# Edge keys as DRAM rows instead of PE transposes, in a two-layer graph kernel on one core

## The chip, the cores and the metric

The program runs on one core of a Trainium2 chip, as one launch. The metric is the time of that launch in device microseconds (us). The time of the kernel before is the median of three runs, 2639.05 us (2638.74 to 2639.62).

## The reference, cut to what matters

Two blocks follow each other on `x` (1250 nodes, 768 features). Each adds to `x` the output of a two-layer graph attention network (GAT) and of a token mixer, both fed by a layer norm of `x`, and then the output of a feed-forward part with chosen experts.

```python
xn = _layernorm(x)
x = x + gnn0(xn, edge_index, ...) + mix0(xn, ...)     # gnn0: 2 GAT layers, 4 heads
x = x + ffn0(_layernorm(x), ...)                      # 2 experts out of 4 for all nodes
xn = _layernorm(x)
x = x + gnn1(xn, edge_index, ...) + mix1(xn, ...)     # gnn1: 2 GAT layers, 1 head
x = x + ffn1(_layernorm(x), ...)
```

A GAT layer does `e = leaky_relu(a_src[src] + a_dst[dst])`, a softmax of `e` over the edges that share a `dst`, and a weighted sum of `h[src]`. There are 21250 edges, `src` and `dst` being int32 arrays of that length, drawn at random, with repeats. The kernel turns the edge list once into a dense matrix of counts (how often an edge occurs), and does every softmax and sum with that matrix.

## The kernel before, in words

Nodes are cut into NT = 10 tiles of T = 125. All five engines run programs of their own, written out in order, and wait for each other on semaphores. PSUM has two rings of banks: five that VectorE (DVE) drains (list `V`) and three that ScalarE (ACT) drains (list `A`); `plan()` writes both lists, and PE and the draining engine walk them in the same order. A bank is filled again only when its entry five (or three) places earlier has been drained.

The start. SP (SyncE's queue) loads `x` in five pieces of two tiles (L2336 to L2341), the value weights W in two halves, the edges as two tiles of 125 partitions by 170 integers, and stores zeros from SBUF over the two count matrices in DRAM (L2346 to L2348). DVE takes the norm's statistics of each piece and normalises it (L1419 to L1432; piece 2 is normalised only after the statistics of piece 3, piece 3 after those of piece 4). PE turns each pair of tiles (L573) and multiplies it with the first half of W (products `("v", t, 0)`), then all tiles with the second half (`("v", t, 1)`). DVE drains the first two products only after piece 4 (L1428 to L1431).

The edge list. An edge's key is `src * 1250 + dst`. The 21250 keys form 170 columns of 125. DVE makes the keys (L1437 to L1440). A scatter with repeated indices would lose additions, so each column is first searched for repeats. For that every partition needs the whole column as a row: PE turns the column, broadcast over 125 columns, into PSUM (`key_rows`, L560 to L568; four columns fill a bank, so there are 43 groups). DVE then compares the row with its own key, once for each column (L1456), which gives how often the key occurs and whether it is the first. Every five groups (20 columns) DVE makes indices and counts (L1469 to L1475) and signals `index_made`. GpSimd (POOL) then adds each column into one of the two count matrices with an indirect DMA, in order, with at most two in flight (L2287 to L2294). It starts only when the zeros are written (L2285).

The 43 groups stand between other PE work: 5 beside the first half of the products v, 12 beside the second (KEYS_BESIDE), 6 in the first block of q and k (KEYS_BESIDE_QK), and 4 after each of heads 0 to 4 (KEYS_AFTER_HEAD).

Then come the eight mixer heads (pk, pq, kv, in some of them a further block of q and k, then num), while POOL scatters. After the heads PE turns the result and makes the first half of GAT layer 0's product (`("h", 0, t, 0)`, L657). For the next stage SP waits until all scatters have landed (L2440), loads the counts (L2443 to L2451), DVE sums them (`count_sum`, L1597 and L1599), and PE turns them into the mask (`mask(j)`, L637) beside the mixer's output product.

The end of GAT layer 1. `gat4` accumulates for each head over ten source tiles j into five banks (L717 to L733). In the last head of layer 1 the last four j are taken bank by bank (L735 to L744, `by_pairs`), so that bank 0 is complete first; in all other heads j is the outer loop. DVE drains a bank, takes statistics, ACT normalises pair by pair (`normalise`, L1041), and PE turns the result for the feed-forward part.

Of the kernel before, what the change touches and what calls it, by code (L numbers as in the profile page):

```python
# [20 lines left out]
F32 = mybir.dt.float32  # L21
# [34 lines left out]
KEYS_BESIDE = [0] * 6 + [2, 3] + [1] * 12  # L56
KEYS_BESIDE_QK = [1] * 6
KEYS_AFTER_HEAD = [4] * 5 + [0] * 3
# [34 lines left out]
def plan():  # L93
# [29 lines left out]

    turned("ln0", range(5))
    keys = [("key", i) for i in range(NKEY)]

    def some_keys(n):
        for _ in range(n):
            V.append(keys.pop(0))

    for half in range(2):
        for t in range(NT):
            V.append(("v", t, half))
            some_keys(KEYS_BESIDE[half * NT + t])

    def qk(b):
        for i, x in enumerate("kq"):
            for c in range(3):
                V.append((x, b, c))
                if b == 0:  # L140
                    some_keys(KEYS_BESIDE_QK[3 * i + c])

    qk(0)
    for h in range(MH):
# [6 lines left out]
        some_keys(KEYS_AFTER_HEAD[h])  # L151
    assert not keys
# [57 lines left out]
def gps_kernel(nc, w, out):  # L210
# [8 lines left out]
    neg_dram = nc.dram_tensor("neg_saved", [T, NT * N], BF16).ap()  # L219
    prow_dram = [nc.dram_tensor(f"target_rows{i}", [2, (H0 - 1) * NT, T], F32).ap() for i in range(2)]  # L220
# [5 lines left out]
    with ctx:  # L226
# [109 lines left out]
        SRCI, DSTI = in_d(EC).bitcast(I32), in_d(EC).bitcast(I32)  # L336
        SRCF, DSTF, KEY, COUNT, FIRSTF, IDXE = (in_d(EC) for _ in range(6))
# [109 lines left out]
        pair_stats, pair_std, pair_normed = sem("pair_stats_made"), sem("pair_std_made"), sem("pair_normed")  # L447
        keys_made, index_made = sem("keys_made"), sem("index_made")
# [57 lines left out]
        def _(pe):  # L506
# [51 lines left out]
            keys = list(range(NKEY))  # L558

            def key_rows():  # L560
                i = keys.pop(0)
                pe.wait_ge(keys_made, 1)
                b = fill("V", ("key", i))
                for j in range(min(KEYG, EC - i * KEYG)):
                    c = i * KEYG + j
                    last = pe.transpose(b[0:T, j * T:(j + 1) * T], KEY[0:T, c:c + 1].to_broadcast([T, T]),
                                        IDENT[0:T, 0:T])
                last.then_inc(v_filled, 1)  # L568

            for half in range(2):  # L570
                for t in range(NT):
# [5 lines left out]
                    for _ in range(KEYS_BESIDE[half * NT + t]):  # L577
                        key_rows()

            def qk(blk):  # L580
                pe.wait_ge(qkw_loaded[blk % 2], 48 * (blk // 2 + 1))
                for i, x in ((1, "k"), (0, "q")):
                    for c, (n0, n) in enumerate(CH):
# [4 lines left out]
                        if blk == 0:  # L588
                            for _ in range(KEYS_BESIDE_QK[3 * (1 - i) + c]):
# [2044 lines left out]
```

## Time and profile before

| | |
|---|---|
| median of 3 runs | 2639.05 us |
| the profiled execution | 2642.76 us, span 2641.0 us |
| PE busy | 2567.0 us (97%) |
| DVE busy | 1586.7 us (60%) |
| ACT busy | 779.6 us (30%) |
| POOL busy | 347.4 us (13%), nearly all of it the 170 scatters |
| DMA | 155.70 MB, mean 59 GB/s |

The profiled execution took 2642.76 us, of which the profile covers 2641.0 us. Times in the rows are us from the start of the span. The view of groups gives for each the busy time, the mean ns of one instruction, and the idle time of the engine just before them with what ended it.

### The profile page before, as it was taken

What the parts mean: (1) busy time and instruction counts of PE and PEld (TensorE: products, weight loads), DVE (VectorE), ACT (ScalarE), POOL (GpSimd) and SP (SyncE); (2) the same over time, 40 slices, a digit from 0 to 9 for tenths busy, and PEclk for the clock granted to TensorE, in tenths of its full rate; (3) what the DMA queues carried; (4) which work ended last, traced back from release to release, by engine and by line L of the source; (5) the groups of instructions that cost most, each with busy time, mean ns of one, the idle gap of its engine ahead of it and who ended that gap; (6) DMA issues with size and microseconds to landing.
All of it is one profiled execution on the core that took longest, in us unless ns stands there. A gap on an engine that the chain in (4) does not pass through costs nothing.

```text
span 2641.0 us, 26830 instructions
## 1 busy us (share of the span) xinstructions
PE 2567.0 (97%) x10673; PEld 1821.8 (69%) x10673; DVE 1586.7 (60%) x2708; ACT 779.6 (30%) x1314; POOL 347.4 (13%) x197
## 2 busy tenths in 40 slices
PE   7999999999999997999999999999999999999999
PEld 4667667558965987777777775465755786556676
DVE  4456471789948996997788998254432461341322
ACT  1043342016732873222222221430002431342000
POOL 0888888000000000000000000000000000000000
PEclk9999999999999998999999999999999999999999
DMA  9232313543020406000120002200350100213201
GB/s 255 23 46 14 50 2 49 142 124 104 20 60 0 106 11 214 1 0 1 72 100 2 24 24 85 99 1 0 97 182 18 36 0 1 59 35 131 86 24 59
DMA packets 138070, 155.70 MB, mean 59 GB/s; under 512 B 96524, under 2 KB 108390, under 8 KB 136418
## 3 DMA queue, kind: packets, MB, share of 16 engines
q1 hardware_dynamic: 67225, 153.56, 18.8%
q0 software_dynamic: 70720, 0.43, 2.8%
q8 instruction: 84, 1.38, 0.2%
q14 instruction: 41, 0.34, 0.0%
HBM read 117.75 MB, written 35.83 MB: 58 GB/s over the span
## 4 chain that ended last, share of the span: by engine, by line
PE 51%; DVE 7%; ACT 2%; issue 1%; DMA 0%; SPq 0%; DVEq 0%; ACTq 0%
PE psum L523 50%; DVE arena L1878 2%; DVE arena L1880 1%; DVE arena L1879 1%; PE psum L534 0%; DVE arena L1871 0%; ACT arena L1140 0%; ACT arena L1145 0%; ACT arena L1031 0%; DVE arena L1536 0%; DVE arena L1944 0%; DVE arena L1378 0%; DVE arena L1877 0%; DVE arena L1870 0%; DVE arena L1903 0%
## 5 line engine op out<-in xcount | busy, mean ns | idle before, releaser
L523 PE MATMUL psum<-arena 128*125 128x384 f32 (+12 forms) x9762 | 2459.8, 413 | 39.0 <-DMA arena<-in_ffn_w 7.1
L523 PEld LDWEIGHTS psum<-arena 128*125 128x125 f32 (+3 forms) x9762 | 1721.0, 188 | 751.5 <-issue 136.4
L2293 POOL DMA_INDIRECT count_matrix<-arena x170 | 342.8, 2016 | 122.8 <-DVE arena L1475 60.9
L1878 DVE RECIPROCAL arena<-arena 128x500 f32<-128x500 f32 x60 | 196.7, 3278 | 2.1
L1628 DVE CUSTOM_DVE_ANT_0 arena<-arena 125x1250 bf16<-125x1250 bf16 (+1 forms) x100 | 139.2, 1457 | 12.9 <-ACT arena L1173 12.3
L2303 POOL MEMSET arena<- 125x60 f32 x1 | 0.2, 207 | 1047.0 <-PE psum L523 1047.0
L1712 DVE TENSOR_TENSOR arena<-arena 125x1250 f32<-125x1250 f32 x80 | 116.3, 1453 | 18.5 <-ACT arena L1122 18.3
L1119 ACT ACTIVATE arena<-arena 125x1250 f32<-125x1250 f32 x80 | 106.9, 1336 | 54.5 <-PE psum L523 54.2
L1715 DVE SCALAR_TENSOR_TENSOR arena<-arena 125x1250 f32<-125x1250 f32 x80 | 116.9, 1461 | 2.8
L1031 ACT ACTIVATE arena<-psum 128x250 f32<-128x250 f32 (+1 forms) x102 | 40.6, 495 | 231.9 <-PE psum L534 231.5
L1265 ACT ACTIVATE arena<-psum,arena 128x250 f32<-128x250 f32 x120 | 49.3, 465 | 198.3 <-PE psum L523 198.3
L1074 ACT ACTIVATE arena<-arena 32x500 f32<-32x500 f32 (+1 forms) x108 | 59.1, 548 | 164.8 <-DVE arena L1509 163.9
L1122 ACT ACTIVATE arena<-arena 125x1250 f32<-125x1250 f32 x80 | 105.8, 1322 | 0.0
L1164 ACT ACTIVATE arena<-psum 125x384 f32<-125x384 f32 x80 | 38.6, 487 | 139.7 <-PE psum L523 139.7
L1257 ACT ACTIVATE arena<-arena 128x500 f32<-128x500 f32 x60 | 37.2, 621 | 140.1 <-DVE arena L1862 139.9
L534 PE MATMUL psum<-arena 125*128 125x125 f32 x420 | 57.7, 282 | 20.1 <-DVE arena L1397 11.3
L1140 ACT ACTIVATE arena<-arena 125x250 f32<-125x250 f32 x100 | 40.4, 490 | 116.5 <-PE psum L523 116.4
L1734 DVE TENSOR_TENSOR arena<-arena 125x2500 f32<-125x2500 f32 x10 | 27.6, 2764 | 72.8 <-ACT arena L1145 72.8
L534 PEld LDWEIGHTS psum<-arena 125*128 125x128 f32 x420 | 45.5, 143 | 33.5 <-issue 19.4
L1646 DVE TENSOR_SCALAR arena<-arena 125x40 f32<-125x40 f32 (+1 forms) x4 | 0.7, 178 | 106.5 <-ACT arena L1164 78.3
L1507 DVE TENSOR_SCALAR arena<-psum,arena 96x500 f32<-96x500 f32 (+1 forms) x36 | 23.3, 647 | 66.0 <-PE psum L523 65.6
L1862 DVE TENSOR_SCALAR arena<-arena 128x500 f32<-128x500 f32 x60 | 25.0, 420 | 60.5 <-ACT arena L1265 59.1
(223 smaller groups left out, 1463.9 us busy)
## 6 DMA issues: line engine op xcount, KB each, us to landing
arena<-in_ffn_w SPq DMA_DIRECT2D x3, 4608.0 KB, 15.4
residual<-arena SPq DMA_DIRECT2D x30, 336.0 KB
arena<-residual SPq DMA_DIRECT2D x30, 336.0 KB
arena<-target_rows SPq DMA_DIRECT2D x12, 610.4 KB
arena<-in_gat_w SPq DMA_DIRECT2D x3, 2304.0 KB, 9.4
arena<-residual SPq DMA_DIRECT2D x10, 672.0 KB
residual<-arena SPq DMA_DIRECT2D x10, 672.0 KB
count_matrix<-arena SPq DMA_DIRECT2D x2, 3125.0 KB, 27.0
```

The costliest lines, as they stand in the source:

```text
L523: return pe.matmul(o, lhsT, rhs, start=start, stop=stop, skip_group_check=share)
L534: last = pe.transpose(b[:, i * T:(i + 1) * T], source[0:T, t0 + i, k * 128:(k + 1) * 128], IDENT[0:T, 0:T])
L1031: act.activation(o, i, ACT.Copy).then_inc(a_drained, 1)
L1074: act.activation(o[low, cols], t[32 * i:32 * i + 32, cols], ACT.Square)
L1119: act.activation(ET4[n % 4][0:T, :], PROWS[layer][h % 2][0][0:T, :], ACT.Exp, bias=ASC[0:T, h, j:j + 1])
L1122: act.activation(E24[n % 2][0:T, :], PROWS[layer][h % 2][1][0:T, :], ACT.Exp, bias=AS2[0:T, h, j:j + 1]).then_inc(slopes_made, 1)
L1265: last = act.activation(HB[u % 2][:, m, :], b[:, j * 250:(j + 1) * 250], ACT.Identity, bias=B1C[:, e, m:m + 1])
L1628: ins = dve.tensor_tensor_reduce(SUMS[n % 2][0:T] if layer < 2 else E24[n % 2][0:T, :], NEG[0:T, t, :], ASROWS[layer][h % 2][0:T, :], 1.0, ...
L1712: dve.tensor_tensor(et, et, E24[n % 2][0:T], ALU.max).then_inc(larger_made, 1)
L1715: dve.scalar_tensor_tensor(et, et, 1.0, CT[0:T, j, :], ALU.min, ALU.mult).then_inc(et_made, 1)
L1878: now(dve.reciprocal(t_, t_))
L2293: pool.indirect_dma_start(counts[k], bass.IndirectOffsetOnAxis(ap=IDX_I[0:T, c:c + 1].bitcast(U32), axis=0), COUNT_I[0:T, c:c + 1], None, ...
```

## The change

Four things are changed.

1. The keys are made in row form. The edges are loaded first of all, as 170 rows of 125 in two parts (128 and 42 partitions), and DVE makes the keys in this form (KEYT) before it looks at `x`. PE turns KEYT once (two transposes), DVE copies the result to the column form KEY that the compares need.
2. KEYT is stored to DRAM (`key_rows`), and each group of four rows is read back by all 125 partitions with one broadcast DMA of up to 250 KB, into one of two buffers in SBUF. The 170 transposes of `key_rows` on PE go away, and DVE compares with a row in SBUF instead of one in PSUM. A load of group i waits until group i - 2 has been used. These loads stand between SP's other loads.
3. The order of SP's first loads is new: edges, x0, first half of W, x1, bias row, KEYT stores, x2, zeros of matrix 0, key rows of groups 0 and 1, x3, zeros of matrix 1, x4, second half of W. The groups are spread differently over DVE's work (5 in the first half of v as before, but beginning two tiles earlier, 7 in the second half, 6 in the first q and k block, 4 after each of heads 0 to 5, 1 after head 6), and the index batches become 2 groups, then ten times 4, then 1.
4. In the last head of GAT layer 1 the order by pairs is gone; it runs as the other heads do. ACT's wait for the last bank moves from pair 3 to pair 0.

```diff
-KEYS_BESIDE = [0] * 6 + [2, 3] + [1] * 12
+KEYS_BESIDE = [0] * 4 + [1, 1] + [1, 1, 1, 0, 1, 1, 0, 1, 1, 0, 1, 1, 0, 1]
 KEYS_BESIDE_QK = [1] * 6
-KEYS_AFTER_HEAD = [4] * 5 + [0] * 3
+KEYS_AFTER_HEAD = [4] * 6 + [1] + [0]
+KEY_BATCHES = [2] + [4] * 10 + [1]
@@ PE
-            def key_rows():
-                i = keys.pop(0)
-                pe.wait_ge(keys_made, 1)
-                b = fill("V", ("key", i))
-                for j in range(min(KEYG, EC - i * KEYG)):
-                    c = i * KEYG + j
-                    last = pe.transpose(b[0:T, j * T:(j + 1) * T], KEY[0:T, c:c + 1].to_broadcast([T, T]),
-                                        IDENT[0:T, 0:T])
-                last.then_inc(v_filled, 1)
+            pe.wait_ge(keyt_made, 1)
+            b = fill("V", ("keyt",))
+            pe.transpose(b[0:T, 0:128], KEYT[:, 0, :], IDENT)
+            pe.transpose(b[0:T, 128:EC], KEYT[0:EC - 128, 1, :], IDENT[0:EC - 128, 0:EC - 128]).then_inc(v_filled, 1)
...
-                    by_pairs = 4 if (layer, h) == (1, H0 - 1) else 0
-                    for j in range(NT - by_pairs):
+                    for j in range(NT):
@@ ACT
-                if stage == 1 and g == 3:
+                if stage == 1 and g == 0:
                     act.wait_ge(v_filled, V_AT[("acc", 1, H0 - 1, 4)] + 1)
@@ DVE
+            dve.wait_ge(edges_loaded, 64)
+            for i, p in parts:
+                step(dve.tensor_copy(SRCTF[p, i, :], SRCT[p, i, :]))
+                step(dve.tensor_copy(KEYT[p, i, :], DSTT[p, i, :]))
+            after(own[0])
+            step(dve.scalar_tensor_tensor(KEYT[:, 0, :], SRCTF[:, 0, :], float(N), KEYT[:, 0, :], ALU.mult, ALU.add))
...
             def key_group():
                 i = keys.pop(0)
-                dve.wait_ge(v_filled, V_AT[("key", i)] + 1)
-                b = bank(("key", i))
+                dve.wait_ge(rows_loaded[i % 2], 16 * (i // 2 + 1))
...
-                    row = b[0:T, j * T:(j + 1) * T]
+                    row = KEY_ROWS[i % 2][0:T, j * T:(j + 1) * T]
@@ SP
+            x_load(0)
+            load(W[:, :, 0:HALF], w["mix0_wv"][:, :, 0:HALF], wv_loaded[0])
+            x_load(1)
+            row_load(0, "mix0_bv", bv_loaded)
+            sp.wait_ge(keyt_made, 1)
+            load(key_dram[0:128], KEYT[:, 0, :], keyt_saved)
+            load(key_dram[128:EC], KEYT[0:EC - 128, 1, :], keyt_saved)
+            sp.wait_ge(zeros_made, 1)
+            x_load(2)
+            zeros_store(0)
+            sp.wait_ge(keyt_saved, 32)
+            key_rows_load(0, 2)
+            x_load(3)
+            zeros_store(1)
+            x_load(4)
+            load(W[:, :, HALF:], w["mix0_wv"][:, :, HALF:], wv_loaded[1])
...
+            key_rows_load(2, 14)
             vf(("v", NT - 1, 1))
-            pieces_load(WS8[:, :, 2 * H0:], w["gat1_w"], gw_loaded[1])
+            pieces_load(WS8[:, :, 2 * H0:], w["gat1_w"], gw_loaded[1], lambda k: key_rows_load(14 + k, 15 + k))
...
                 block_load(blk)
+                if blk > 2:
+                    key_rows_load(4 * blk + 8, 4 * blk + 12)
+            key_rows_load(28, 32)
...
             block_load(5)
+            key_rows_load(32, NKEY)
```

## Rows read from the trace of the kernel before

**Rows 1.** The page, parts 1 and 4: busy times, and the chain by engine.
```profile
PE 2567.0 (97%) x10673; PEld 1821.8 (69%) x10673; DVE 1586.7 (60%) x2708; ACT 779.6 (30%) x1314; POOL 347.4 (13%) x197
...
PE 51%; DVE 7%; ACT 2%; issue 1%; DMA 0%; SPq 0%; DVEq 0%; ACTq 0%
```
**Rows 2.** Groups by line, the key transposes: busy us, mean ns, idle before them.
```profile
L566 PE MATMUL psum<-arena 125*125 125x125 f32 x170 | 23.4, 274 | 4.0 <-DVE arena L1562 4.0
```
**Rows 3.** Timeline where PE waits for the counts: start us, us, engine, [idle before].
```profile
64.46 2.14 POOL L2293 DMA_INDIRECT count_matrix<-arena  x1 [60.90 <-DVE arena L1475]
...
83.56 1.98 POOL L2293 DMA_INDIRECT count_matrix<-arena  x1 [0.30 <-issue]
...
467.12 1.99 POOL L2293 DMA_INDIRECT count_matrix<-arena  x1 [0.30 <-issue]
...
477.27 0.29 DVE L1599 TENSOR_TENSOR arena<-arena 125x125 f32<-125x125 f32 x1
...
477.82 1.72 PE L642 MATMUL psum<-arena 125*125 125x125 f32 x10 [2.17 <-DVE arena L1599]
```
**Rows 4.** Timeline of DVE in the first 80 us.
```profile
22.23 1.02 DVE L1378 BATCH_NORM_STATS2 arena<-arena 125x6 f32<-125x384 f32 x2 [2.13 <-DMA arena<-in_x]
...
26.12 1.01 DVE L1378 BATCH_NORM_STATS2 arena<-arena 125x6 f32<-125x384 f32 x2
...
30.33 1.01 DVE L1414 TENSOR_TENSOR arena<-psum,arena 125x384 f32<-125x384 f32 x2
...
62.32 0.18 DVE L1469 TENSOR_SCALAR arena<-arena 125x20 f32<-125x20 f32 x1
...
74.52 0.56 DVE L1414 TENSOR_TENSOR arena<-psum,arena 125x384 f32<-125x384 f32 x1 [2.68 <-PE psum L523]
...
76.06 0.08 DVE L1456 DVE_READ_ACCUMULATOR arena<-psum,arena 125x1 f32 x1
```
**Rows 5.** Busy times by stretch: PE, PEld, DVE, ACT, POOL, PEclk, DMA share, GB/s.
```profile
20.00:24.00 4.00, 4.00 (x12) 2.21 (x11) 1.84 (x6) 0.20 (x1) 0.00 (x0) 1.00 1.07 239
...
32.00:36.00 4.00, 4.00 (x14) 2.31 (x13) 0.00 (x0) 0.00 (x0) 0.00 (x0) 1.00 1.02 410
```
**Rows 6.** Timeline of SP's queue: the issue of the zeros.
```profile
12.44 14.03 SPq L2319 DMA_DIRECT2D count_matrix<-arena  x2
```
**Rows 7.** Timeline of PE in the products v.
```profile
16.23 10.46 PE L523 MATMUL psum<-arena 128*125 128x384 f32 x24 [0.47 <-ACT arena L1031]
...
39.08 8.01 PE L523 MATMUL psum<-arena 128*125 128x384 f32 x24 [0.47 <-ACT arena L1031]
...
66.06 4.04 PE L523 MATMUL psum<-arena 128*125 128x384 f32 x12
...
70.38 4.04 PE L523 MATMUL psum<-arena 128*125 128x384 f32 x12
```
**Rows 8.** Timeline of POOL: scatters that were held up or took longer.
```profile
135.67 1.99 POOL L2293 DMA_INDIRECT count_matrix<-arena  x1 [1.11 <-DMA count_matrix<-arena]
...
328.19 2.33 POOL L2293 DMA_INDIRECT count_matrix<-arena  x1 [0.31 <-issue]
```
**Rows 9.** Waits up to 500 us: who for whom, us in total, times, longest.
```profile
DVE arena L1552 <- PE psum L523: 42.5, 8, 12.6
...
POOL count_matrix L2293 <- DMA count_matrix<-arena: 15.4, 19, 2.1
```
**Rows 10.** Stretches in which the granted clock (PEclk) fell.
```profile
478.00:482.00 4.00, 4.00 (x15) 2.76 (x15) 3.97 (x6) 0.00 (x0) 0.00 (x0) 0.58 0.76 203
...
999.00:1002.00 3.00, 3.00 (x14) 3.00 (x14) 0.50 (x3) 0.20 (x1) 0.00 (x0) 0.69 0.66 211
```
**Rows 11.** Timeline of the last head of GAT layer 1.
```profile
995.09 14.18 PE L523 MATMUL psum<-arena 125*125 125x193 f32 x68 [1.95 <-DVE arena L1715]
...
1001.47 0.17 DVE L1674 RECIPROCAL arena<-psum 125x2 f32<-125x2 f32 x1 [2.46 <-PE psum L523]
...
1009.31 0.17 DVE L1674 RECIPROCAL arena<-psum 125x2 f32<-125x2 f32 x1 [0.23 <-PE psum L523]
```

## Prediction of the time after the change

> **What bounds the kernel now.** I read the page's busy times and the chain first. PE is busy 97% of the span and makes 51% of the chain [rows 1], so in most stages a microsecond less of PE is a microsecond less of time. The groups by line then price what PE loses: the 170 key transposes are 23.4 us busy, with 4.0 us of waits before them [rows 2]. Whether that is a gain must be read where the edge list is consumed, and there the timeline says something else [rows 3]. PE is free for the mask at 475.65 and waits 2.17 us, for the sum of the counts. Followed back: PE 477.82, count sum 477.27, and, with the load of the counts between, the last scatter at 467.12, 10.7 us before PE. POOL's 170 scatters run as a chain of their own: the first starts at 64.46, the ninth at 83.56, so eight take 19.1 us or 2.39 each; and in the whole chain (467.12 - 64.46)/169 = 2.38. In 2.38 each there are 15.4 us of waits for the scatter before last to land [rows 9]. So up to 478 us two chains end within 2.2 us of each other, PE's and POOL's. The change shortens PE's. The time follows POOL's, which no part of it makes faster: only an earlier start of the scatters counts, less what the new DMAs and compares cost them.
>
> **PE's chain.** It loses 23.4 + 4.0 = 27 us at most and gets two transposes (0.27 each) and the stalls at the start worked out below, some 7 us. It would be ready for the mask near 475.65 - 27 + 7 = 456 while the counts come near 477, and what lies between is cover: up to some 20 us of new stalls on PE before the mask cost nothing. Under that cover I put DVE's waits for key rows after the heads (four groups in a row, two buffers, so the third and fourth wait for a load each, a few us for a head). Before, DVE waits 42.5 us in 8 for the kv product [rows 9], about 5 a head, so most of it is hidden twice. If the cover were gone it could cost up to 10 us.
>
> **When the scatters can start.** The zeros, 2 x 3125 KB, go out at 410 GB/s [rows 5]: 15.6 us. Their issue alone holds SP for 14 us [rows 6], long before DMA gets to them, so SP's new waits for the keys and for their store leave the DMA engines fed. The DMA share is 1.0 and above in the first 60 us [rows 5], so what is put ahead of a load delays it by its bytes.
> - x3 is waited for until 22.23; x4 (750 KB at 239 GB/s, 3.2 us) is thus there by about 25.6, just before DVE takes it at 26.12 [rows 4, 5].
> - In the change there stand before x4, besides: the zeros 15.6, two key row loads of 250 KB at the rate of x, 2.0, the store of the keys (85 KB) 0.5, the edges (170 KB, 0.7 by bytes; four issues and their landing ahead of x0 may double it) 1.5. x4 lands at 25.6 + 19.6 = 45.2, with 1.5 either way.
> - DVE drains product v(0) only after x4's statistics and the norm of piece 3: 30.33 + 0.5 - 26.12 = 4.75 us behind x4 [rows 4], so at 50.0. The list V has the entry keyt at its head now, so v(5) is the first product that needs this bank. It started at 39.08 + 3.92 = 43.0 [rows 7] and now starts at 50.0.
> - The start of PE's products moves too: x1 stands behind half of W (1152 KB, 4.7 us), and PE's first product, 16.23 [rows 7], moves to about 21. From there v(5) would be due at 47.8, so x4 is the later of the two and decides.
> - From v(5) to v(0, second half) it is 70.38 - 43.0 = 27.4 us, less seven key groups at 4.32 - 3.92 = 0.4 each [rows 7], so 24.5: it starts at 74.5. DVE drains it 4.14 us later and has compared group 5 1.6 us after that (74.52 to 76.14) [rows 4]: 80.3.
> - Group 5 completes the second batch of indices. From the last compare to the scatter it takes 64.46 - 62.32 = 2.14 us [rows 3, 4]: 82.4.
> The first batch (2 groups, 8 columns) is ready after v(5), some 57 us, 7 us earlier than 64.46, but lasts only 8 x 2.29 = 18.3 us, so POOL stands still from about 75 to 82.4. What counts is the ninth scatter: 82.4 against 83.56, 1.2 us earlier. Later batches (16 columns, 37 us) are ready in time: groups 6 to 17 come with v and the first q and k, by 140 us, and four for a head after that, while POOL takes 4 groups in 38 us and a head takes 22 to 46.
>
> **What the scatters pay.** Two costs that the trace shows only beside other work.
> - The 41 row loads that run beside them. A late landing holds up the next scatter but one. All large transfers beside the scatters now cost 15.4 us together [rows 9], some 60 transfers, which is 0.25 each at most and gives 10 us; below, nothing (a delay of less than some 0.9 us, 2 x 2.29 less 3.7 to land, is not seen). The nearest rows are the twelve 192 KB pieces of GAT weights, one every 2.4 us from 113 us on, beside which one scatter waited 1.11 us instead of 0.30 [rows 8]: 0.07 a piece, 2.8 for 41. The row loads stand further apart; I take half, 1.4 us, ends 0 and 10.
> - The compares read both tensors from SBUF now, 170 x 0.27 = 46 us of DVE time. The scatter at 328.19 took 2.33 us in place of 1.99, beside DVE additions of two SBUF tensors [rows 8]. One such hit of 0.34 for each of 41 groups would be 14 us. But POOL's whole busy time less 170 x 1.99 leaves 9 us [rows 1], the constants included, for every hit that DVE's additions make now, and these are twice as long as a compare. I take three hits, 1.0, ends 0 and 14.
> The Trainium skill speaks against this part: "SBUF — State Buffer", section "SBUF: two separate sides", says that a VectorE operation with two SBUF inputs and a GpSimd operation that reads SBUF lock the same pair of ports, and the later one waits for the whole of the other. By that rule most compares could hold a scatter for their whole length, the second rival below. The trace agrees in kind (2.33) and, so far, not in size.
>
> **Sum to the mask.** -1.2 + 1.4 + 1.0 = +1.2 us.
>
> **The clock after a longer wait.** Now PE waits 2.17 us, and the granted clock is 0.58 in 478 to 482 [rows 10]: 3.4 us at the lower level (1.2 GHz), which cost 1.7. In the change PE waits some 20 us. The nearest case is 995.09 [rows 11], after 7 us of mostly idle PE: there 0.69 in 999 to 1002 [rows 10] puts the end of the lower level at 1000.9, 5.8 us after the restart, a loss of 2.9. So 0 to +1.2 more than now; I take +0.7.
>
> **The last head.** By pairs, PE idles until the last weights are made, falls to the lower clock, and ends its last 68 matmuls at 1009.3 [rows 11]. Less the 2.9 us lost to the clock they take 0.166 each, so in plain order, where PE follows the weights j by j (20 matmuls, 3.3 us), it ends one to two j behind the last weights, near 1001. But DVE and ACT set what follows: the banks are drained every (1009.31 - 1001.47)/3 = 2.61 us, with 0.23 idle before the last [rows 11], which is the round of drain, deviation and ACT's norm. In plain order the first bank comes near 999, the second is due 2.6 us later, near 1001.5 as now, and the round goes on at 2.61. So 0, from -0.6 to +2.7 (the transposes that follow at the low clock, since PE now idles just before them); I take +0.3. Nothing covers this stage: all engines wait on that chain.
>
> **Sum.** 1.2 + 0.7 + 0.3 = +2.2 us on the profiled execution, 2642.76, which stands 3.7 us above the median of the runs; on the median it gives 2639.05 + 2.2 = 2641.3 us.
>
> **The rivals.**
> - *The scatters do start earlier* (0.15). For it: half of the zeros no longer stand before anything that PE needs early. If x4 did not hold v(5) back, the product v(0, second half) would come from the start of PE alone, 16.23 to 21, and start between 67 and 72; the ninth scatter at 75 to 80, 4 to 8 us earlier. With the costs above 2634, without them 2632. Against it: the DMA share is 1.0 all along, and DVE's order ties v(0)'s drain to x4.
> - *Scatters slowed by compares and row loads* (0.22), the slower side. Place: the 400 us of scatters; price 0.25 us more for each of 41 groups or row loads, +10 us: 2651. It decides from about 0.1 a group, where the sum passes 5 us. Against it are the nearest rows, nearly all of which show unharmed scatters.
> - *PE's chain is the bound after all* (0.03). Then 27 - 7 = 20 us are gained, 2619. It needs the counts to be ready before 457, which no chain here allows.
> - *The last head turns slower* (0.05), at the low clock, +2.7 in place of +0.3: 2643.7.
>
> **How the numbers follow.** My forecast has 0.55. Its own range is 2637 to 2646 (x4 1.5 us either way, the costs halved or doubled, the tail). With the rivals the range is 2633 to 2650. Within 0.2%, 5.3 us, which is about what a measurement of this kernel can tell from no change, lies most of the forecast (0.45), part of the first rival (0.05) and the fourth (0.03): 0.53. Faster by more: 0.15 (rest of the first, the third, a little of mine). Slower by more: 0.32 (the second, and the upper end of my own).
>
> **What would show it.** In the profile after: PE idle some 15 to 25 us before the first mask transposes, released by the count sum; POOL starting near 57, standing still before its ninth scatter, which begins at 81 to 84; x4's statistics near 45 and v(5) waiting on DVE's drain; scatters mostly at 1.99 with few longer. A last scatter before 462 or after 472, or no wait of PE before the mask, would make the forecast wrong.

## The result, and the profile after

The changed kernel takes 2670.31 us (median of four, 2667.94 to 2675.43) beside 2639.34 us for the kernel before (2638.74 to 2641.9). The ratio is 1.0118, 95% interval 1.0104 to 1.0133: 31 us slower, outside the forecast range. The profiled execution took 2670.43 us with a span of 2668.7 us. A single profile is one execution; the one of before stands some 3 us above its median, and the last scatter of one and the same chain can move by 2 us from profile to profile (see the plain last head below).

The timelines of GpSimd, VectorE and TensorE after the change, to be read against [rows 3] and [rows 4]: start, duration, engine, operation, and in brackets the idle time before it and what ended it.

```profile
5.30 0.55 PE L557 MATMUL psum<-arena 128*125 128x128 f32 x1 [5.30 <-DVEq L1399]
...
21.82 10.24 PE L520 MATMUL psum<-arena 128*125 128x384 f32 x24 [0.47 <-ACT arena L1002]
...
47.49 1.02 DVE L1349 BATCH_NORM_STATS2 arena<-arena 125x6 f32<-125x384 f32 x2 [8.23 <-DMA arena<-in_x]
...
51.98 4.13 PE L520 MATMUL psum<-arena 128*125 128x384 f32 x12 [3.40 <-DVE arena L1385]
...
60.05 2.14 POOL L2274 DMA_INDIRECT count_matrix<-arena  x1 [56.49 <-DVE arena L1455]
...
68.85 1.98 POOL L2274 DMA_INDIRECT count_matrix<-arena  x1 [4.38 <-DMA count_matrix<-arena]
...
84.63 1.98 POOL L2274 DMA_INDIRECT count_matrix<-arena  x1 [0.41 <-issue]
...
444.83 39.77 PE L520 MATMUL psum<-arena 128*125 128x392 f32 x120 [0.47 <-ACT arena L1002]
...
495.85 1.99 POOL L2274 DMA_INDIRECT count_matrix<-arena  x1 [0.30 <-issue]
...
505.81 0.29 DVE L1579 TENSOR_TENSOR arena<-arena 125x125 f32<-125x125 f32 x1
...
506.36 2.44 PE L625 MATMUL psum<-arena 125*125 125x125 f32 x10 [21.76 <-DVE arena L1579]
```

The front came out nearly as forecast. The fifth input piece is taken at 47.49 us, v(5) starts at 51.98, and the ninth scatter at 84.63 (before: 83.56). The last scatter, however, starts at 495.85 in place of 467.12 [rows 3], 28.7 us later, and the mask 28.5 us later. From the mask on little is different. The whole loss lies between the ninth scatter and the last, 411.2 us in place of 383.6.

The groups of the page after the change (busy time, mean ns; then idle time before):

```profile
L2274 POOL DMA_INDIRECT count_matrix<-arena x170 | 343.3, 2019 | 151.0 <-DVE arena L1455 56.5
...
L1436 DVE SCALAR_TENSOR_TENSOR arena<-arena 125x125 f32<-125x125 f32 x170 | 49.5, 347 | 44.1 <-issue 29.2
```

And two waits of GpSimd and TensorE (us in all, times, longest):

```profile
POOL count_matrix L2274 <- DMA count_matrix<-arena: 54.7, 40, 4.4
...
PE psum L520 <- issue: 11.8, 3, 5.7
PE psum L520 <- ACT arena L1056: 7.2, 1, 7.2
```

The scatters themselves are no longer than before (2.02 us each). They wait for earlier scatters to land: 54.7 us in place of 15.4 [rows 9], 39.3 us more, of which 6 lie before the ninth.

TensorE did not get early to the mask either. It is free at 444.83 + 39.77 = 484.60 us, not at 456, although its 23.4 us of transposes [rows 2] are gone. Two stretches of the busy table show why (TensorE's busy time, clock, DMA share, GB/s), first before, then after:

```profile
0.00:120.00 120.00, 104.33 (x387) 1.00 0.61 146
120.00:440.00 320.00, 309.96 (x1485) 0.99 0.32 36
```
```profile
0.00:120.00 120.00, 96.27 (x314) 1.00 0.65 171
120.00:440.00 320.00, 299.10 (x1348) 0.96 0.39 60
...
146.00:160.00 14.00, 9.06 (x16) 0.52 0.51 81
256.00:263.00 7.00, 6.28 (x35) 0.58 0.14 3
409.00:416.00 7.00, 6.02 (x31) 0.54 0.46 81
...
488.00:512.00 24.00, 5.64 (x17) 0.52 0.49 105
```

Idle time rises by 104.33 - 96.27 = 8.1 us in the front and by 309.96 - 299.10 = 10.9 us behind it; with 0.5 us more behind 440 it is 45.2 us in place of 25.7 up to where TensorE is free, 19.5 more. In each of three stalls (7.2, 5.7 and 5.6 us) the granted clock had fallen to 1.2 GHz, from 2.4, before TensorE went on, and stayed there for a while: 0.52, 0.58 and 0.54 are 13.4, 5.9 and 6.4 us at the low level. Only the part in which TensorE works costs anything. In the first stretch it works for 9.06 us of 14. The busy time of each microsecond times what its clock lacks of 1.00 sums up to 9.6 us (before, in one spell from 147 to 151 us, 1.7 us), 7.9 us more.

So 19.5 + 7.9 = 27.4 us are lost, and TensorE was only 8.95 us later (484.60 against 475.65). Taking the transposes off, less the two new ones, gave 18.4 us back, not 23.4. The reason stands in the prediction's own reading of [rows 7], where a group of four lengthens TensorE's chain by 4.32 - 3.92 = 0.4 us: 43 groups are 17.2 us; the other 1.2 us stay open. The 23.4 us of the view of groups count time that overlaps the products beside them.

### The profile page after: what moved, and what is told of

The parts are those of the page before. It is cut to its first block, busy times and chain, and to the rows that moved or that the text cites. A ratio compares the mean times of both kernels' runs of the same rounds, so it can differ in the third digit from the quotient of the medians.

```text
span 2668.7 us, 26524 instructions
## 1 busy us (share of the span) xinstructions
PE 2557.8 (96%) x10505; PEld 1812.7 (68%) x10505; DVE 1591.8 (60%) x2730; ACT 780.0 (29%) x1314; POOL 347.9 (13%) x197
## 4 chain that ended last, share of the span: by engine, by line
PE 51%; DVE 7%; ACT 2%; issue 1%; DMA 0%; SPq 0%; DVEq 0%; ACTq 0%
PE psum L520 50%; DVE arena L1858 2%; DVE arena L1859 1%; DVE arena L1860 1%; PE psum L531 0%; DVE arena L1851 0%; ACT arena L1111 0%; ACT arena L1116 0%; ACT arena L1002 0%; DVE arena L1516 0%; DVE arena L1924 0%; DVE arena L1349 0%; DVE arena L1857 0%; DVE arena L1850 0%; DVE arena L1883 0%
## 5 line engine op out<-in xcount | busy, mean ns | idle before, releaser
L2274 POOL DMA_INDIRECT count_matrix<-arena x170 | 343.3, 2019 | 151.0 <-DVE arena L1455 56.5
L1608 DVE CUSTOM_DVE_ANT_0 arena<-arena 125x1250 bf16<-125x1250 bf16 (+1 forms) x100 | 139.2, 1458 | 12.6 <-ACT arena L1144 12.3
L1436 DVE SCALAR_TENSOR_TENSOR arena<-arena 125x125 f32<-125x125 f32 x170 | 49.5, 347 | 44.1 <-issue 29.2
L1714 DVE TENSOR_TENSOR arena<-arena 125x2500 f32<-125x2500 f32 x10 | 27.6, 2764 | 72.8 <-ACT arena L1116 72.8
```

Of the source, the lines that this page charges most:

```text
L1436: ins = dve.scalar_tensor_tensor(EQL[c % 2][0:T], row, KEY[0:T, c:c + 1], LOWER[0:T], ALU.is_equal, ALU.mult, accum_out=COUNT[0:T, c:c + 1])
L1608: ins = dve.tensor_tensor_reduce(SUMS[n % 2][0:T] if layer < 2 else E24[n % 2][0:T, :], NEG[0:T, t, :], ASROWS[layer][h % 2][0:T, :], 1.0, ...
L2274: pool.indirect_dma_start(counts[k], bass.IndirectOffsetOnAxis(ap=IDX_I[0:T, c:c + 1].bitcast(U32), axis=0), COUNT_I[0:T, c:c + 1], None, ...
```

## The experiments

My theory after the result was this: a row load writes 125 partitions, and its packets go to 5 of the 16 DMA engines only, which hold the scatters' packets up. The Trainium skill, "DMA: Bandwidth & Descriptors", section "Why a DMA increments its semaphore by 16 and not by 1", says that a transfer uses the largest number of engines up to 16 that divides the slowest dimension of both its sides, which is 5 for 125 and 16 for 128. The busy table agrees (GpSimd's busy time, clock, DMA share, GB/s). These are two picked microseconds in which row loads run, first in the changed kernel, then in the version with 128 partitions:

```profile
202.00:203.00 1.00, 1.00 (x1) 1.00 0.38 104
203.00:204.00 1.00, 0.47 (x1) 1.00 0.34 96
```
```profile
197.00:198.00 1.00, 1.00 (x1) 1.00 0.63 166
198.00:199.00 1.00, 0.92 (x1) 1.00 1.03 195
```

At 100 GB/s only about a third of the engines' time is taken, which fits five full engines and eleven nearly idle ones. No view used here names the engine of a packet, so the number five is the page's rule and the table agrees with it.

**Loads over 128 partitions.**

```diff
-load(KEY_ROWS[i % 2][0:T, 0:n * T], row.to_broadcast([T, n * T]), ...)
+load(KEY_ROWS[i % 2][:, 0:n * T], row.to_broadcast([128, n * T]), ...)
```


> The changed kernel with one edit: each key row load writes all 128 partitions in place of 125, the same data for three more partitions, so that its packets can be dealt to 16 DMA engines in place of 5. Theory (narrow loads): 125 packets of 2000 B on 5 engines keep each of these busy for about 2.2 us a load, 8 to 10 us when four follow one another, and the scatters' packets on these engines wait; on 16 engines a load takes 0.7 us. Then GpSimd's waits for scatters to land fall from 54.7 us to about 20, the last scatter starts near 462 to 472 in place of 495.85, and the kernel takes 2642 to 2652 us. Rival (bytes): the 10 MB of row loads are what holds the scatters; then as many bytes cost as much, and the last scatter stays within 5 us of 496, the time near 2670. Rival (port lock, compares from SBUF): no change either, 2670.

Measured: 2651.12 us (2647.75 to 2653.01), ratio 1.0043 (1.0028 to 1.0059).

```profile
83.66 1.98 POOL L2274 DMA_INDIRECT count_matrix<-arena  x1 [0.71 <-DVE arena L1455]
...
435.93 39.77 PE L520 MATMUL psum<-arena 128*125 128x392 f32 x120 [0.47 <-ACT arena L1002]
...
473.16 1.99 POOL L2274 DMA_INDIRECT count_matrix<-arena  x1 [0.30 <-issue]
...
483.82 2.43 PE L625 MATMUL psum<-arena 125*125 125x125 f32 x10 [8.12 <-DVE arena L1579]
```

Three more partitions, with 2% more bytes, take 19 us off: from the ninth scatter to the last it is 389.5 us in place of 411.2. Both rivals fall: the compares still read SBUF, and the bytes are no fewer. 6 us stay, and GpSimd's landing waits are 32.4 us, more than the 20 I expected. TensorE is free at 475.70 us, no sooner than before the change, so making the loads free would not win 27 us either. The profiled execution is the fastest of its four, 3.4 us below their median, so the 5.9 us that stay may be too few: with the third buffer below, 11.7 stay.

**No loads at all.**

```diff
-for i in range(first, last):
-    if i >= 2:
-        sp.wait_ge(rows_used, i - 1)
+for i in range(first, min(last, 2)):
```


> The changed kernel without the key row loads of groups 2 to 42: those groups compare with the rows of groups 0 and 1, every scatter goes to the trash rows, and the count matrices start as ones (so the mask is another). Compares read SBUF as often as in the changed kernel; 41 loads and every wait for them are gone. Theory (the loads are the whole cost of the scatters): GpSimd's chain runs at 2.29 to 2.35 each, last scatter at 450 to 462 (it starts at 60), and TensorE is ready for the mask 20 us or more before its 484.6 in the changed kernel, since VectorE no longer waits; time 2630 to 2642 us. Rival (compares from SBUF cost scatters): last scatter 10 us or more later than that, above 470, and GpSimd's mean scatter above 2.05 us. Rival (TensorE's chain is long for another reason, VectorE's compares no longer covered by the transposes): ready for the mask still after 470.

A first form of this run, with the scatters left as they are, gave no result, since with such compares a scatter can hold an index twice. So here every scatter goes to the 125 entries behind the matrix, and the matrices start as ones; the numbers that come out are not the reference's.

This gave another answer than it was made for. It took 3711.74 us (3699.91 to 3720.06): all 170 scatters now add to the same 125 entries (of one or the other matrix in turn), and nearly each waits for the one before last to land, 1094.6 us in 155 waits.

```profile
200.03 1.98 POOL L2274 DMA_INDIRECT count_matrix<-arena  x1 [6.22 <-issue]
208.00 1.99 POOL L2274 DMA_INDIRECT count_matrix<-arena  x1 [5.99 <-DMA count_matrix<-arena]
```

A scatter takes (1526.06 - 61.59)/169 = 8.7 us in place of 2.4, and TensorE stands 83.5 us for a weight load besides. It tells nothing of the loads' price or of TensorE's chain. What it shows is a price for scatters into these entries. They are the same ones each time and also lie side by side in memory, two bytes each; which of the two makes them slow was not tried.

**Every compare twice**, on the version with 128 partitions.

```diff
+scratch[2 + c % 2] = step(dve.scalar_tensor_tensor(EQL[2 + c % 2][0:T], row, KEY[0:T, c:c + 1], LOWER[0:T],
+                          ALU.is_equal, ALU.mult, accum_out=FIRSTF[0:T, c:c + 1]))
```


> The version with 128-partition loads, every compare done twice (the second result unused): 170 more VectorE operations that read two SBUF tensors, 46 us. Theory (no port lock worth telling): GpSimd's busy time stays within 2 us of 341.5 and the last scatter within 4 us of 473. VectorE then holds up the kv copies, four groups after a head taking 4.6 us more, so TensorE loses 10 to 25 us before the mask and the time is 2660 to 2670 us. Rival (each such compare can hold a scatter): GpSimd's busy time grows by 10 us or more.

Measured: 2656.96 us (2652.77 to 2659.84), ratio 1.0058 (1.0041 to 1.0075).

```profile
L2277 POOL DMA_INDIRECT count_matrix<-arena x170 | 343.2, 2019 | 138.7 <-DVE arena L1458 63.9
```

GpSimd is busy 343.2 us beside 341.5: 46 us more of such VectorE operations make the scatters 1.7 us longer. That is no lock of any size. The last scatter, at 483.46, came 10.3 us later where I allowed 4: 3.1 us of it by the first start (63.27 against 60.15), the rest by later indices and by waits. TensorE is free at 447.00 + 39.77 = 486.77, 11.1 us later and so at the low end of the 10 to 25 that I expected. The median rose by 6 us only, not 10 to 20. The two profiles are of the slowest execution of its four and of the fastest of the other four, so their differences may be too large. The 1.7 us are also little more than GpSimd's busy time moves by itself (341.5 with two row buffers, 342.7 with three).

**Every load nearly twice**, on the same version.

```diff
+if 2 <= i < NKEY - 1:
+    load(EXTRA[i % 2], row[:, 0:420].to_broadcast([128, 420]), rows_loaded[i % 2])
```


> The version with 128-partition loads, each of 40 row loads followed by a second of 420 elements a partition (84% of its bytes) into memory that nothing reads. Theory (what is left of the cost, 6 us of late last scatter, is these loads' own bytes on the 16 engines): the last scatter comes 4 to 12 us after 473, the time is 2655 to 2665 us. Rival (what is left comes from the front of the kernel or from elsewhere): last scatter within 2 us of 473.

Measured: 2680.64 us (2676.39 to 2683.73), ratio 1.0153 (1.0136 to 1.017); last scatter 505.83, which is 32.7 us later.

```profile
POOL count_matrix L2275 <- DMA count_matrix<-arena: 62.6, 43, 5.5
```

So the loads' own traffic costs on 16 engines too, and steeply: the 41 single ones some 6 us, 84% more bytes right behind them 33 us. My upper end was 12, and 2665 for the time.

**Half loads**, on the changed kernel with its 125 partitions.

```diff
-load(KEY_ROWS[i % 2][0:T, 0:n * T], ...)
+for c0 in range(0, n, 2):
+    c1 = c0 + 2
+    if c0:
+        sp.wait_ge(rows_loaded[i % 2], 32 * (i // 2) + 16)
+    load(KEY_ROWS[i % 2][0:T, c0 * T:c1 * T], ...)
```


> The changed kernel (125 partitions, 5 engines) with each row load cut in two of half its bytes, the second issued when the first has landed. Theory (length of hold against slack): two scatters take 4.6 us and one lands in 3.7, so a scatter that is held up less than some 0.9 us costs nothing; a whole narrow load holds its 5 engines 2.2 us and costs 1.3 us, a half holds them 1.1 us and costs 0.2 at most, though the engines move as many bytes. Then GpSimd's landing waits fall from 54.7 us to 20 to 32 and the last scatter from 495.85 to 470 to 480. VectorE gets its rows some 4 us later each, so TensorE's chain may be later than 484.6, and the time near 2665. Rival (the cost goes by the engines' time or bytes in all): waits stay above 45 us, last scatter above 488.

Measured: 2681.87 us (2680.04 to 2683.34), ratio 1.0151 (1.0136 to 1.0167). Ninth to last scatter 400.7 us (changed kernel 411.2, 128 partitions 389.5), landing waits 44.5 us in 51. The last scatter starts at 494.84, only 1 us earlier than in the changed kernel, since the ninth starts at 94.17, 9.5 us later.

```profile
POOL count_matrix L2274 <- DMA count_matrix<-arena: 44.5, 51, 2.7
```

Neither theory holds alone. As many bytes on as few engines cost the scatters 10 us less when cut and spaced, so length matters, but the waits stayed near the rival's 45, and the last scatter is where the rival had it (after 488). The rest of the time is VectorE's waits for its rows, 102.6 us in all, which put TensorE behind the scatters.

**A third row buffer**, with 128 partitions.

```diff
-KEY_ROWS = [mem(edges_at, KEYG * T), in_d(KEYG * T)]
+KEY_ROWS = [mem(edges_at, KEYG * T), in_d(KEYG * T), mem(edges_at + KEYG * T, KEYG * T)]
```


> The version with 128-partition loads and a third row buffer, so that the third of four groups after a head no longer waits for its load. Theory (VectorE's waits for rows are part of what delays TensorE): VectorE's waits at the compares fall from 21.5 us to under 12, TensorE is ready for the mask at 466 to 472 in place of 475.7; the scatters' chain, which ends later, is as before (last scatter 471 to 475), so the time stays at 2647 to 2652 us. Rival (the waits hide behind others): ready within 2 us of 475.7.

Measured: 2655.74 us (2652.91 to 2658.13), ratio 1.0052 (1.0036 to 1.0067). VectorE's waits at the compares fell from 27.5 to 12.3 us, and TensorE was free for the mask at 432.96 + 39.77 = 472.73, 3 us earlier, between my 466 to 472 and the rival's 473.7. From the ninth scatter to the last it is 395.3 us, 11.7 more than before the change. The scatters, loads unchanged in size, ended 8 us later than with two buffers (481.09), which no theory of mine expects: earlier loads may collide more, or it is the spread of single executions.

**Earlier scatters**, with 128 partitions and three buffers: three groups compared before the fifth input piece.

```diff
+                if i == 3:
+                    for _ in range(3):
+                        key_group()
```


> A version meant to beat both: 128-partition loads, a third row buffer, and the first three key groups compared while VectorE waits for the fifth input piece, so that the scatters can start when the zeros are there, near 44 us in place of 60. If the scatters keep up, the last starts near 458 to 465 and TensorE's chain (475.7 us in the version with 128-partition loads, some us less with the third buffer) sets the mask at 468 to 476 in place of 477.8 before: time 2630 to 2638 us. Rival: the early scatters wait behind the input pieces (two waited 4.0 us each at 62 to 68), gain half, and TensorE's chain stays at 476: 2638 to 2642 us.

Measured: 2645.20 us (2641.97 to 2649.45), ratio 1.0022 (1.0012 to 1.0031). Both my range and the rival's (up to 2642) were too low. Against the version with 128 partitions the first scatter starts at 44.58, 15.6 us earlier, the ninth 15.5 us, but the 25th only 7 us and the last 5.6 us.

```profile
44.58 2.13 POOL L2277 DMA_INDIRECT count_matrix<-arena  x1 [41.02 <-DMA count_matrix<-arena]
...
73.11 1.99 POOL L2277 DMA_INDIRECT count_matrix<-arena  x1 [2.96 <-DMA count_matrix<-arena]
75.40 2.06 POOL L2277 DMA_INDIRECT count_matrix<-arena  x1 [0.30 <-issue]
81.77 1.99 POOL L2277 DMA_INDIRECT count_matrix<-arena  x1 [4.31 <-DMA count_matrix<-arena]
84.06 1.99 POOL L2277 DMA_INDIRECT count_matrix<-arena  x1 [0.30 <-issue]
```

I took the stop before 81.77 for a wait for the second batch of indices, which VectorE has ready at 77.6 us, and the expectation of the next run says so. That was a misreading. The first batch is three groups, 12 scatters, and these four lines are the 10th to the 13th. The 10th and the 12th, both of the first batch, stand 2.96 and 4.31 us until an earlier scatter has landed; the 13th, the first that needs the second batch, follows with the usual 0.30.

So it is no surprise that cutting that batch to two groups did not help:

```diff
-KEY_BATCHES = [3] + [4] * 10
+KEY_BATCHES = [3, 2] + [4] * 9 + [2]
```


> The version with early scatters (128-partition loads, third row buffer, first three groups before the last input piece), the second batch of indices cut to two groups so that it is ready before GpSimd has used up the first. In the version before, the second batch came at 77.6 us where GpSimd stood from 72.2. Expected: the last scatter at 460 to 464 in place of 467.5, the mask at 470 to 473 (TensorE's chain is free at 469.5), TensorE's wait there under 3 us in place of 8.4, and the time 2634 to 2640 us. Rival (what is gained at the front is lost again in waits behind the row loads): mask after 476, 2642 us and more.

Measured: 2645.59 us (2639.45 to 2650.96), ratio 1.0013 (1.0004 to 1.0022). The rival held: in the profile, which is the slowest execution of the eleven, the last scatter is at 474.16 and the mask at 484.84.

**Rows for the first groups only**, the other 40 or 35 groups turned by TensorE as before.

```diff
+ROW_GROUPS = 3        # and 8
+by_rows = i < ROW_GROUPS
```


> A version that keeps of the change what paid: the new front (keys in row form, zeros between the input pieces), row loads over 128 partitions for the first three key groups alone, compared before the last input piece, and the plain last head; the other 40 groups are turned by TensorE into PSUM as before. No row load runs beside the scatters after the first. Expected: first scatter near 45, scatters at 2.38 each as before plus some 8 us of waits behind the input traffic, last scatter 450 to 460; TensorE, with 12 transposes fewer, is ready for the mask at 472 to 476 and does not wait there: mask at 472 to 476 in place of 477.8, no low clock behind it (1.5 us), head 1 us: 2632 to 2637 us. Rival (the front holds TensorE back by as much as is gained): 2638 to 2642 us.

> As e11_rows_first3, with the first eight groups by row loads, five of them beside the first scatters. Against e11: TensorE makes 20 transposes fewer (2.7 us), the scatters meet five more loads of 256 KB between 45 and 80 us (0.2 to 1 us each). TensorE is ready at 470 to 474; if that bounds, the time is 1 to 3 us below e11's. Rival (VectorE's waits for the rows hold TensorE's banks): equal to e11 or above.

Measured: 2648.38 us (2645.58 to 2652.25), ratio 1.0036 (1.0022 to 1.0050), with 3; 2646.27 us (2643.88 to 2648.22), ratio 1.0020 (1.0010 to 1.0029), with 8. With 3 groups:

```profile
51.62 5.83 PE L534 MATMUL psum<-arena 128*125 128x384 f32 x12 [4.72 <-DVE arena L1419]
...
443.05 39.77 PE L534 MATMUL psum<-arena 128*125 128x392 f32 x120 [0.47 <-ACT arena L1036]
483.47 1.35 PE L659 MATMUL psum<-arena 125*125 125x125 f32 x10 [0.65 <-ACT arena L1169]
```

The scatters are free of the trouble: ninth to last 383.5 us, as before (383.6), last at 453.69. TensorE, without any wait for the counts, comes to the mask 5.7 us later than before, with 12 transposes fewer. It is free at 443.05 + 39.77 = 482.82 in place of 475.65, and the transposes should have given back a microsecond or so: 8 to 9 us is what the new front costs TensorE here. Of these its idle time in the first 120 us shows 7.9 (23.6 us in place of 15.7). Even my rival (2638 to 2642) was too good. With 8 groups the median is 2.1 us lower, as expected in number, but the two intervals overlap, and TensorE is free at 484.75 us, not at 470 to 474.

**The plain last head**, alone, on the kernel before.

```diff
-by_pairs = 4 if (layer, h) == (1, H0 - 1) else 0
-for j in range(NT - by_pairs):
+for j in range(NT):
```


> The kernel before with one part of the change: the last head of the second GAT layer in plain order (with ScalarE's wait at the first group of the norm). By the changed kernel's trace, where the way from the last weights to the first logits product is 2.4 us shorter, this gains 1.5 to 2.4 us: 2637 us. My recorded forecast for this part was +0.3 (-0.6 to +2.7): 2639.5.

Measured: 2638.39 us (2637.38 to 2642.93), ratio 0.9996 (0.9987 to 1.0005): no difference that can be told from none.

```profile
476.03 1.35 PE L642 MATMUL psum<-arena 125*125 125x125 f32 x10 [0.65 <-ACT arena L1152]
```

The profile shows one thing more. TensorE does not wait for the counts here, and the last scatter starts at 464.99, 2.1 us before that of the kernel before, though the edit touches nothing ahead of either. In the kernel before the two chains are so close that the single execution decides which of them ends last.

**A shorter first batch of indices**, on that version.

```diff
-if i % 5 == 4 or i == NKEY - 1:
+if i + 1 in [sum(KEY_BATCHES[:k + 1]) for k in range(len(KEY_BATCHES))]:    # [2, 3] + [5] * 7 + [3]
```


> The kernel before with the plain last head and the first batch of indices cut from five key groups to two (then 3, 5, ...), so that GpSimd can start near 59 us in place of 64.5. No front order, no row loads. Expected: if the early scatters are not held up, the last scatter comes 3 to 5 us earlier, the counts no longer decide, TensorE starts the mask at 475.7 to 476.2 without a wait, and the time is 2634 to 2638 us. Rival (until 68 us the input traffic holds each scatter up, as in the changed kernel, where a start 4.4 us earlier had been lost by the ninth scatter): the ninth scatter stays near 83, mask and time as in e3_plain_head, 2637 to 2639 us.

Measured: 2637.64 us (2635.1 to 2639.02) beside 2641.00 us, ratio 0.9987 (0.9978 to 0.9996), 3.4 us faster than the kernel before, with both edits.

```profile
56.55 2.14 POOL L2283 DMA_INDIRECT count_matrix<-arena  x1 [52.99 <-DVE arena L1464]
...
65.86 1.98 POOL L2283 DMA_INDIRECT count_matrix<-arena  x1 [0.30 <-issue]
...
457.35 1.99 POOL L2283 DMA_INDIRECT count_matrix<-arena  x1 [0.30 <-issue]
...
472.77 1.35 PE L643 MATMUL psum<-arena 125*125 125x125 f32 x10 [0.65 <-ACT arena L1153]
```

The scatters start at 56.55 us (before 64.46), hold all of it, and the last starts 9.8 us earlier. The rival, by which the ninth would stay near 83, fell: it starts at 75.02. TensorE never waits for the counts. In this execution, the fastest of the eleven, it was itself 3.3 us early (free at 472.12, 475.38 in the version without the edit), and the edit has no part in that. Its first product, at 15.8 us, took 9.04 us in place of 10.61, and the spell at the low clock from 147 to 151 us, which costs 1.7 us in the profiles of the kernel before and of the plain head, did not come, though the stall of 2.85 us just ahead of it is the same in all three.

This version is faster than both kernels. Whether the shorter batch adds to the plain head is not resolved: the intervals of the two ratios overlap (0.9978 to 0.9996 and 0.9987 to 1.0005), and in both profiles TensorE reaches the mask without a wait.

## Why the prediction was wrong, step by step

- **Which chain ends last.** Right: the time follows GpSimd's chain, TensorE stands 21.76 us before the mask.
- **When the scatters can start.** Right in the path through x4 and v(5), a little off in size, and in part by luck. x4 was taken at 47.5 (forecast 45.2, 1.5 either way), v(5) ran at 52.0 (50.0), the ninth scatter started at 84.63 (82.4). GpSimd started at 60.05, not 57, and what held it before the ninth was landing waits (6.9 us in all), not a missing index: the second batch was ready at 83.7 us, before the eighth scatter was done.
- **What the row loads cost the scatters.** This step failed. I took 1.4 us with 10 as the upper end, from 192 KB pieces on 128 partitions [rows 8]. It was 27.6 us from the ninth scatter to the last. Size and number of the transfers were right; their shape was not looked at. Of these 27.6 us, 21.7 go when the loads write 128 partitions and 5.9 stay, inside my 0 to 10; with the third buffer, in another single profile, 11.7 stay. The medians say the same of the larger part, 2670.31 against 2651.12. That the scatters' packets queue behind the loads' on shared engines is the explanation that fits; shown are the effect of the partitions and that of cutting the loads. My bound of 10 us came from all large transfers of the kernel before, none of them so long on so few engines beside the scatters. The second rival (+10 us) had the place, not the mechanism and a third of the price.
- **Compares from SBUF.** 1.0 us forecast. GpSimd is busy 343.3 us, and 341.5 with 128 partitions and the same compares; doubling them adds 1.7. The Trainium skill's rule of the shared ports ("SBUF — State Buffer", section "SBUF: two separate sides"), by which a VectorE operation with two SBUF inputs can hold a GpSimd operation that reads SBUF for its whole length, does not show on these scatters in size: 170 more compares are 46 us, and 1.7 of them were seen on GpSimd.
- **TensorE's chain.** Its front stalls were forecast at 7 us and were 8.1. The rest failed: I put it 20 us ahead of the mask and called that cover for at most 10 us of stalls. Taking the transposes off, less the two new ones, was worth 18.4 us, not 27 (23.4 busy and 4.0 of waits). Stalls behind the front rose by 10.9 us where 4.0 should have gone, and the clock after them cost 7.9 us more, which I had not priced at all before the mask. The transposes after a head had themselves been cover: while TensorE made them, VectorE did its compares. Without them VectorE compares four groups, with waits for rows, and only then makes the weights and the copy that TensorE waits for. Two runs show the share of the row waits: loads over 128 partitions bring TensorE from 484.60 to 475.70 us, the third buffer to 472.73. That the rest is the lost cover is argued from the timelines, not tried alone. The second of the three stalls is an example. VectorE waits for rows, compares and makes indices until 251.8, then makes 17 of the score weights, and only then the copy (L1532) that TensorE, idle since 251.05, waits for:

```profile
251.79 0.36 DVE L1516 CUSTOM_DVE_ANT_0 arena<-arena 128x192 f32<-128x192 f32 x1
...
256.26 0.36 DVE L1532 COPY arena<-psum 128x194 f32<-128x194 f32 x1
...
256.72 5.52 PE L520 MATMUL psum<-arena 128*125 128x97 f32 x26 [5.68 <-issue]
```

- **The clock after the longer wait.** +0.7 forecast. After 21.76 us of waiting the granted clock is 0.52 in 488 to 512. From the mask to the logits (the product that scores the four experts) it is 1046.97 - 506.36 = 540.6 us after, and 1014.52 - 476.03 = 538.5 in the version with the plain head alone, which did not wait: 2.1 us for the clock, against 1.7 in the kernel before [rows 10], so +0.4. Right.
- **The last head.** +0.3 forecast with -0.6 as the lower end; by the trace it is -1.9 us at the logits (1046.97 - 506.36 = 540.6 against 1020.30 - 477.82 = 542.5), and -2.3 without the clock's +0.4; 1.0 us is lost again behind them. The round of 2.61 us was not a constant. After the change the five drains of the last group of banks run at 2.34 each, and the second comes 2.13 us after the first, not 2.6:

```profile
1026.44 0.17 DVE L1654 RECIPROCAL arena<-psum 125x2 f32<-125x2 f32 x1 [2.27 <-PE psum L520]
1028.57 0.16 DVE L1654 RECIPROCAL arena<-psum 125x2 f32<-125x2 f32 x1
...
1035.80 0.16 DVE L1654 RECIPROCAL arena<-psum 125x2 f32<-125x2 f32 x1
```

In the time alone it isn't resolved (0.9996).

Two terms were mis-sized: the scatters beside the row loads (1.4 us, measured 27.6), and TensorE's chain, which I put 20 us ahead of the mask and which ends 6.8 us behind the old one (484.60 against 477.82). The first alone decided the time. Without it the second would have: TensorE alone would have set the mask at about 485, 7 us later than before; by this estimate the kernel would have taken some 2646 us, the upper end of my own range. Both have one root in part: with 128 partitions the rows also reach VectorE sooner, and TensorE is free at 475.70. That is still no gain on the 475.65 of before, so what was taken off TensorE had come to nothing by the mask.

## What to carry to other kernels

Before pricing a DMA that runs beside latency-bound small ones, work out on how many engines its shape puts it: 125 partitions and 128 are nearly the same bytes and not the same transfer. Price what is taken off an engine by how much it lengthens the chain, not by its busy time where it overlaps its neighbours. Work taken off the critical engine may have been the cover of another engine, so follow that other engine's order through the gap before counting the removal as a gain, and price the clock after each new stall. When a chain is bound by its start, try the smallest first batch before rebuilding what feeds it: with one changed list the last scatter started 9.8 us earlier, and with the plain head the kernel gained 3.4 us, where the rebuilt front lost.

## What the runs showed of the hardware

- Loads of 250 KB beside a chain of scatters cost 0.67 us each when they write 125 partitions (27.6 over 41), and 0.14 us (5.9 over 41, two buffers) to 0.29 us (11.7 over 41, three buffers) when they write 128; 210 KB more behind each adds 0.8 us. Each figure is from one profile.
- 170 scatters that add to the same 125 neighbouring entries of DRAM take 8.7 us each, against 2.4 on spread ones.
- Three stalls of 5.6 to 7.2 us on TensorE, behind the front, ended at the lower clock: 25.7 us of it, which cost 9.6 us. Stalls of 6.2 and 5.9 us in the first 20 us did not (1.00 throughout), and after one and the same stall of 2.85 us the low clock came in two profiles and not in a third. The length of a stall alone doesn't tell.
